# Solving product and output product of a gated delta rule: batch 0 first, with the wait for the product in front at batch 1 alone

## The reference

```python
Sk = einsum('bhkv,bhk->bhv', S, k_t)
delta = einsum('bhv,bhk->bhkv', v_t, k_t) - einsum('bhv,bhk->bhkv', Sk, k_t)
S = exp(g_t)[..., None, None] * S + b_t[..., None, None] * delta
o_t = einsum('bhkv,bhk->bhv', S, q_t)
```

## Time and profile before

| | us |
|---|---|
| median of 3 runs | 1865.31 (1857.83 to 1867.53) |
| profiled execution, its own time | 1864.56 |
| profiled execution, span | 1862.1 |
| mean granted TensorE clock | 0.943 |
| TensorE busy | 1599.3 |
| VectorE busy | 1196.3 |

### The profile page before, as it was taken

One profiled execution on the slowest core, in us unless ns is written; L12 is line 12 of the kernel. 1 busy time (PEld: TensorE's weight loads), 2 busy tenths in 40 slices (PEclk: granted clock), 3 DMA queues, 4 the chain that ended last, 5 costly groups with the idle time before them and its releaser, 6 DMA issues. The chain is left out here.

```text
span 1862.1 us, 75918 instructions
## 1 busy us (share of the span) xinstructions
PE 1599.3 (86%) x32268; PEld 1190.0 (64%) x32268; DVE 1196.3 (64%) x3029; ACT 807.2 (43%) x1898; POOL 966.8 (52%) x1197
## 2 busy tenths in 40 slices
PE   6579999999999999999999998757999995799950
PEld 6235666666666666666666666647888885788840
DVE  1488888888888888888888888313555553222214
ACT  1355565565565565566556555211111111233313
POOL 0144544544554554554554544203777776677853
PEclk9889999999999999999999999658999998899985
DMA  6354665565565665655655564415555541698557
GB/s 267 95 104 102 124 130 124 126 128 121 130 131 124 128 129 123 130 125 125 132 126 121 119 129 99 94 33 185 151 176 153 171 153 50 185 263 225 95 91 240
DMA packets 565042, 253.97 MB, mean 136 GB/s; under 512 B 458321, under 2 KB 532689, under 8 KB 563809
## 3 DMA queue, kind: packets, MB, share of 16 engines
q1 hardware_dynamic: 412640, 209.15, 43.4%
q10 hardware_dynamic: 133632, 20.98, 6.2%
q0 software_dynamic: 18432, 18.99, 5.8%
HBM read 177.68 MB, written 71.37 MB: 134 GB/s over the span
## 5 line engine op out<-in xcount | busy, mean ns | idle before, releaser
L376 PE MATMUL delta_p_j<-delta_xt,delta_w 128*128 128x512 f32 x768 | 385.9, 627 | 23.6 <-DMA delta_xt<-in_xt 18.3
L593 DVE SCALAR_TENSOR_TENSOR delta_kq<-delta_hist,cw,delta_kq 128x512 f32<-128x512 f32 x384 | 290.7, 757 | 29.9 <-ACT delta_kq L745 22.8
L910 POOL TENSOR_TENSOR delta_sd<-state,eg_end 128x256 f32<-128x256 f32 x128 | 128.5, 1004 | 276.5 <-DVE state L675 275.8
L1271 POOL DMA_INDIRECT slot_tokens<-mix_tokens,mix_slot x192 | 189.7, 988 | 62.5 <-issue 62.2
L376 PEld LDWEIGHTS delta_p_j<-delta_xt,delta_w 128*128 128x128 f32 x768 | 132.5, 192 | 134.5 <-issue 119.7
L738 ACT ACTIVATE delta_hist<-delta_p_j 128x512 f32<-128x512 f32 x192 | 114.1, 594 | 233.8 <-PE delta_p_j L376 223.2
L879 POOL TENSOR_SCALAR delta_n<-delta_n 128x8 f32<-128x8 f32 x64 | 15.4, 241 | 263.6 <-DVE delta_n L624 263.6
L794 ACT ACTIVATE delta_kpv<-delta_kpv,delta_root 128x64 f32<-128x64 f32 x512 | 135.7, 343 | 16.3 <-ACT delta_xit L780 16.3
L1365 PE MATMUL expert_p_h<-expert_xbt,w 128*88 128x128 f32 x1024 | 127.0, 278 | 10.2 <-ACT expert_xbt L1408 9.1
L1365 PEld LDWEIGHTS expert_p_h<-expert_xbt,w 128*88 128x88 f32 x1024 | 115.7, 158 | 28.2 <-ACT expert_xbt L1408 23.1
L1059 PE MATMUL mix_p_y<-mix_wo,mix_ot 128*128 128x256 f32 x512 | 120.0, 389 | 13.8 <-DMA mix_wo<-in_wo 13.8
(11 more groups left out here) (147 smaller groups left out, 3643.3 us busy)
## 6 DMA issues: line engine op xcount, KB each, us to landing
delta_xd<-x_scratch SPq DMA_DIRECT2D x256, 128.0 KB
delta_w<-in_wqkv SPq DMA_DIRECT2D x64, 416.0 KB
w<-in_w SPq DMA_DIRECT2D x64, 352.0 KB
delta_eg<-eg_rows SPq DMA_DIRECT2D x128, 130.0 KB
n_scratch<-delta_kkq ACTq DMA_DIRECT2D x128, 128.0 KB
mix_ot<-ot SPq DMA_DIRECT2D x16, 1024.0 KB
w<-in_w SPq DMA_DIRECT2D x64, 176.0 KB
delta_xd<-x_scratch SPq DMA_DIRECT2D x128, 64.0 KB
```

Of the source, the lines that this page charges most:

```text
L376: mm = pe.matmul(view(p_j, 512 if n == 2 else 0, (1, 512)), w[e][:, (ch * 3 + n) * 128:(ch * 3 + n) * 128 + 128], xt[m // 8 % 2][:, ch * 5 ...
L593: ve.scalar_tensor_tensor(out, view(hist[e], i * 2 * 518 + tap, (259, 2), (1, 256)), cw[:, column:column + 1], out, ALU.mult, ALU.add).the ...
L910: po.tensor_tensor(view(sd, 0, (128, 2), (C, 2), (1, C)), view(state, first_pair(group) * 128, (C, 2), (128, 2), (1, C)), view(s.eg_end, g ...
L1271: po.indirect_dma_start(out=s.tok.ap(), out_offset=bass.IndirectOffsetOnAxis(ap=slot[i % 2][:, k:k + 1], axis=0), in_=tokens[:, i:i + 1], ...
```

## The change

In `chain_solve` and in `chain_update` the loops over q and b are exchanged, so that batch 0's four matmuls come first and batch 1's four after them, and the wait for the product in front stands between the two.

```diff
--- before.py
+++ after.py
@@ -504,9 +504,10 @@
                 if c == 0:
                     pe.wait_ge(tt_out, group * 2 + 2)
                     pe.wait_ge(first_out, group * 2 + 2)
-                pe.wait_ge(qs, 8 * n + 8)
-                for q in range(2):
-                    for b in range(NB):
+                for b in range(NB):
+                    if b == 1:
+                        pe.wait_ge(qs, 8 * n + 8)
+                    for q in range(2):
                         for sh in range(2):
                             mm = pe.matmul(view(p_c, b * 512 + 128 + q * C, (1, C), parts=half(sh)),
                                            view(kkq, ring(group * 2 + q) + b * 256 + c * C, (1, C), parts=half(sh)),
@@ -528,9 +529,10 @@
                 mm.then_inc(ds, 1)
                 if c == 0:
                     pe.wait_ge(masked, group * 2 + 2)
-                pe.wait_ge(ds, n + 1)
-                for q in range(2):
-                    for b in range(NB):
+                for b in range(NB):
+                    if b == 1:
+                        pe.wait_ge(ds, n + 1)
+                    for q in range(2):
                         for sh in range(2):
                             mm = pe.matmul(view(p_c, b * 512 + 384 + q * C, (1, C), parts=half(sh)),
                                            view(u, (b * 2 + q) * C, (1, C), parts=half(sh)),
```

## The result

The changed kernel takes 1841.05 us (median of 4 runs, 1837.1 to 1843.5) against 1866.42 for the kernel before beside it: a ratio of 0.9865 [0.9821, 0.9909], 25 us saved. The profiled execution took 1840.0 us against 1864.6 before.

A forecast was written before the change was run, and what follows sets the result against it. TensorE's in-order stream was taken to set the pace in most places, VectorE a close second. Odd slots 29.6, even slots 12.9 and last steps 8.4 us, less 4.3, give 46.6 off 1864.6: 1818 us, range 1800 to 1838.

The forecast's parts named there:

- What a wait saves: In L511 and L535, four pairs instead of eight are left behind each wait's release, saving 0.23 us each.
- Rival C: The wait's release moves, batch 1 starting 0.44 us after batch 0: no change, 1865 us; chance 0.08.
- rival D: Four pairs in a row to one bank serialize: a product costs 0.21 us more, 1918 us; chance 0.04.
- Even slots: Even slots of the recurrence: first half gains nothing, second half 0.46 us, together 12.9 us over 28 slots.
- The place of the wait: Even slots' first half: TensorE's wait for VectorE's update appears at L488 in every slot, some 0.5 us.
- Odd slots: Odd slots of the recurrence (7 to 63) keep all of the gain, 1.02 us each, 29.6 us over 29 slots.
- the deduction: 10% off the odd and even slots' gains, 4.3 us, for slots where something else is late already.
- the first two terms: The gains of the odd slots, 29.6 us, and of the even slots, 12.9 us.
- Last steps: Last seven slots (14 steps), recurrence alone at the lower clock: 0.6 us a step, between 0.46 and 0.87; 8.4 us.
- A: All of the gain counts, even slots' 12.9 us more and no deduction: 1801 us; chance 0.10.
- B: VectorE takes the even slots whole, so only odd slots and the end count: 1830 us; chance 0.15.

The follow-up runs named there:

- order_only: Kernel before with the new loop order in both products, but both waits still ahead of batch 0: 1865.69 us against 1865.91, ratio 0.9991.
- both: Changed kernel with GpSimd's weighting and VectorE's reciprocal moved earlier, odd slots' row lengths first, and the reordering of spread: 1828.06 us, 0.9771 of the kernel before.
- spread: Changed kernel with the value projection's second part (L376) ahead of the inverse's first products (L441) on TensorE, ScalarE's order to match: 1832.15 us, 0.9786 of before.
- pad64: Changed kernel with 64 more TensorE instructions (16 small matmuls) ahead of the recurrence: 1839.53 us, 0.9841 of the kernel before.
- lengths_first: Changed kernel with VectorE's reduction of the squares ahead of the first two rows of the odd slots' inverse: 1838.41 us, 0.9825 of the kernel before.

## Why the prediction was partly right

**What a wait saves** was right: 0.24 and 0.22 us against 0.23, L512 at 0.04 (0.06 forecast), and batch 1 released as before, 0.44 and 0.31 us after the last matmul of the product in front. Rival C falls by the timeline. That the order costs nothing is shown by order_only, and rival D falls with it. The Trainium skill's rule on row tiles and one PSUM bank (TensorEngine Tiling, Restrictions and Gotchas, PSUM Pressure), read as rival D has it, would have made this kernel slower; no run here shows a cost.

**Even slots** were right: first half 7.70 to 7.71 and second half -0.47, against nothing and -0.46. The place of the wait was only partly right: a gap of over 0.2 us right ahead of L488 is there in 9 of 28 even first halves, for 1 before. In 18 of the other 19 TensorE had lost time already, at L472 just ahead of the slot's first step or in a pause within the half.

**Odd slots and the deduction** are where it failed. "Odd slots keep all of it: 0.92 + 0.10 = 1.02" was true of the best of them (0.64 + 0.47 = 1.11) and not of the median (0.24 + 0.01). The step that failed is the deduction for it: "In a few slots something else is late already ... I take 10% of the first two terms off, 4.3". The runs show 28.9 us in its place: the pauses grew by 18.2 and the waits ahead of L472 by 10.7. The first two terms less the deduction were to give 38.2 us, and the stretch gave 17.1. I had asked what is late next only of waits with a releaser in the view, and VectorE's idle time in the odd slots had satisfied me. Missing were the pauses under "issue", which the trace of before has 18 times, and GpSimd's weighting, which used VectorE's idle time before the update; I had taken the other engines' instructions at durations that did not depend on when they run.

**Last steps** were right within what executions differ by. In this pair the last 14 steps gave 10.4 us for 8.4, but the granted clock differed too (0.68 and 0.77). Over all profiled executions they took 96.3 us on average in the six without the change and 88.9 in the nine with both products changed: 7.4 us. At the lower clock a step gains 0.80, near the upper bound of 0.87, because the gap there is wide enough for the four pairs and the release stands as it did.

**Rivals A and B**: the measured saving is smaller than either's (1801 and 1830 us were their times). B's mechanism, VectorE taking the even slots whole, is not what happened, since their second half gained. What came about is a mix that no case held: gains as in the forecast, with a loss over all slots.

**What is shown and what is argued.** Shown: the pauses stand at a fixed place in blocks of 256 instructions, end 1.0 to 1.7 us after the queue's last packet has landed, fall with lighter DMA traffic in three pairs of kernels, and account with the waits ahead of L472 for the missing 29 us. That 13 us more are to be had with both exchanges is shown by the run both. spread has fewer pauses in both kernels, by 13.1 and 3.9 us, where pad64 alone is 7.7 us from the kernel after: that density makes them is likely, not shown. Its time is barely apart from the kernel after's (0.9816 and 0.9821 are the nearest ends of the intervals) and not from pad64's. Shown too is that the growth of L609's time is all beside GpSimd's weighting. Argued only: how much of the waits ahead of L472 comes from this and how much from the transfer of kb (5.3 to 12.3 us); lengths_first shortened the second alone, by 3.7 us, and L472's waits did not follow, but that is too small a change to decide it.

## What to carry to other kernels

Where a change makes the busiest engine's stream shorter by a constant in every round, count the places where that engine paused with no releaser, and what ran in the idle time of the second busiest engine; both grow first. And try the change again after relieving them: here 25 us became 32 or 38, by how it is counted. A wait for one's own earlier product costs less by the work that does not need it and is issued ahead of it: here 0.23 us of a gap of 0.44 and of one of 0.32.

## What was not expected of the hardware

**The program's supply.** TensorE paused 39 times, by 0.75 us on average, at the end of a 256-instruction block. The three shown in the trace around 886, 920 and 954 us used their block up in 3.3 to 3.4 us and ended 4.0 to 4.5 us after it began, 1.4 to 1.5 us after the packet had landed. A slot uses up 3.5 blocks in some 17 us, but unevenly: blocks of 64-wide matmuls (0.06 us a pair) run ahead of the supply, and long ones (L376, 0.43 us apart) leave it time. Lighter DMA traffic (99 instead of 127 GB/s from 154 to 1110 us) halved the pauses, and the packets landed 0.23 us sooner.

**VectorE beside GpSimd.** A tap of L609 takes 0.75 us alone; the two that start 0.76 us ahead of the end of L894 take 0.46 us more than the two of before that start 0.30 ahead. The Trainium skill (SBUF — State Buffer, SBUF: two separate sides) says that a VectorE instruction with two SBUF inputs and a GpSimd instruction that reads SBUF share a port pair, and the later one is held until the other has ended. The rows agree: both delta_hist and delta_yv are in SBUF, and the extra time is the extra overlap, 0.76 - 0.30 = 0.46. Narrow windows of the timeline show the taps one by one, first before, then after:

```profile
816.35 0.85 DVE L607 SCALAR_TENSOR_TENSOR delta_yv<-delta_hist,cw,delta_yv 128x512 f32<-128x512 f32 x1
...
817.23 0.99 DVE L607 SCALAR_TENSOR_TENSOR delta_yv<-delta_hist,cw,delta_yv 128x512 f32<-128x512 f32 x1
```
```profile
874.81 1.32 DVE L609 SCALAR_TENSOR_TENSOR delta_yv<-delta_hist,cw,delta_yv 128x512 f32<-128x512 f32 x1
...
876.16 0.99 DVE L609 SCALAR_TENSOR_TENSOR delta_yv<-delta_hist,cw,delta_yv 128x512 f32<-128x512 f32 x1
```

Each ends 0.55 us (to 0.01) after the GpSimd instruction in whose time it began: the first taps after L892 and L894, which end at 816.65 and 875.57, the second ones after L910 and L912, which end at 817.68 and 876.60. Counted over the stretch of the kernel after, 103 of 112 taps end 0.55 us after such an end, and the other nine take 0.75. The first 0.20 us of a tap's 0.75 are thus not added to the hold (an estimate, 0.75 - 0.55).
